# Attention and feed-forward block on one core: probabilities of the longest row of tiles transposed by DMA from SyncE

## The reference

```python
y = x * rsqrt(mean(x * x) + 1e-6) * rms_w
q, k, v = split(y @ w_in.T)                    # 8 groups: 4 x 64, 64, 64 columns each
q, k = rope(q), rope(k)
qk = where(causal, q @ k.T * 64 ** -0.5, -inf)
o = softmax(qk) @ v
x1 = layernorm(x + (x + o @ w_out.T))
x_q = ternary(x1, 0.33, 0.5)
out = layernorm(x1 + x_q @ (ternary(weight, 0.2, 0.6) + rram_variation).T)
```

## Time and profile before

| | us |
|---|---|
| median of 2 timed runs | 1411.64 (1410.79 to 1412.50) |
| the profiled execution | 1411.72 |
| its span | 1409.9 |
| TensorE busy | 1289.2 (91%) |
| VectorE busy | 1182.2 (84%) |
| ScalarE busy | 1107.8 (79%) |
| GpSimd busy | 852.2 (60%) |

### The profile page before, as it was taken

One profiled execution on the slowest core, in us unless ns is written; L12 is line 12 of the kernel. 1 busy time (PEld: TensorE's weight loads), 2 busy tenths in 40 slices (PEclk: granted clock), 3 DMA queues, 4 the chain that ended last, 5 costly groups with the idle time before them and its releaser, 6 DMA issues.

```text
span 1409.9 us, 25319 instructions
## 1 busy us (share of the span) xinstructions
PE 1289.2 (91%) x7328; PEld 755.6 (54%) x7328; DVE 1182.2 (84%) x3062; ACT 1107.8 (79%) x2327; POOL 852.2 (60%) x904
## 2 busy tenths in 40 slices
PE   4689898999989999999989999999989999898886
PEld 2455555555645555555645555555555555454554
DVE  4688887989898898988898898989898898888976
ACT  5768778788888888788888888788887788687764
POOL 1356666386746765386646766386646766786566
PEclk9799999999999999999999999999999999999998
DMA  6101111021101201021101211021101211110012
GB/s 202 26 20 48 56 31 32 27 57 46 39 21 47 59 28 31 25 59 45 38 22 42 59 33 31 24 61 43 37 24 28 71 35 44 56 42 27 19 36 82
DMA packets 45164, 61.82 MB, mean 44 GB/s; under 512 B 10465, under 2 KB 27105, under 8 KB 45025
## 3 DMA queue, kind: packets, MB, share of 16 engines
q1 hardware_dynamic: 45024, 60.20, 14.4%
HBM read 34.74 MB, written 4.46 MB: 28 GB/s over the span
## 4 chain that ended last, share of the span: by engine, by line
PE 53%; POOL 10%; DVE 9%; issue 9%; ACT 8%; DMA 7%; SPq 3%; POOLq 0%; DVEq 0%; ACTq 0%
PE s L1167 11%; PE x L1179 11%; PE t L1223 11%; PE x L1207 7%; PE ot L1138 6%; DMA spread<-recip_rows 6%; PE ot L1136 5%; ACT prob L831 4%; DVE prob L1010 3%; DVE prob_lo L1102 2%; ACT prob_hi L799 2%; POOL o_raw L766 2%; SPq L574 1%; POOL o_lo L772 1%; SPq L590 1%
## 5 line engine op out<-in xcount | busy, mean ns | idle before, releaser
L799 ACT ACTIVATE prob_hi<-t 128x512 f16<-128x512 f32 x576 | 340.3, 592 | 139.4 <-PE t L1223 134.5
L1102 DVE SCALAR_TENSOR_TENSOR prob_lo<-t,prob_hi 128x512 f16<-128x512 f32 x576 | 394.2, 685 | 59.7 <-ACT prob_hi L799 53.9
L831 ACT ACTIVATE prob<-prob,neg_max 128x896 f32<-128x896 f32 (+7 forms) x512 | 391.9, 767 | 9.3 <-DVE neg_max L1010 7.3
L1167 PE MATMUL s<-k_t,q_t 128*128 128x512 f16 (+3 forms) x1536 | 349.5, 329 | 32.7 <-DVE neg_max L1010 12.1
L1223 PE MATMUL t<-ident,prob 128*128 128x128 f32 x2304 | 350.3, 275 | 6.8 <-ACT prob L831 6.7
L1010 DVE CUSTOM_DVE_ANT_0 prob<-s,mask,score_scale 128x512 f32<-128x512 f32 (+3 forms) x512 | 319.8, 643 | 41.1 <-PE s L1167 23.9
L1223 PEld LDWEIGHTS t<-ident,prob 128*128 128x128 f32 x2304 | 289.4, 142 | 105.8 <-ACT prob L831 14.0
L1138 PE MATMUL ot<-prob_lo,v_sb 128*128 128x512 f16 x576 | 220.7, 383 | 30.2 <-DVE prob_lo L1102 29.1
L1136 PE MATMUL ot<-prob_hi,v_sb 128*128 128x512 f16 x576 | 220.1, 382 | 1.5 <-DVE o_raw L1083 0.9
L1167 PEld LDWEIGHTS s<-k_t,q_t 128*128 128x128 f16 x1536 | 137.7, 99 | 123.1 <-DVE neg_max L1010 37.6
L772 POOL TENSOR_TENSOR o_lo<-o_raw,o_hi 128x256 f16<-128x256 f32 x128 | 86.2, 674 | 194.1 <-ACT o_hi L906 192.5
(11 more groups left out here) (105 smaller groups left out, 1816.5 us busy)
## 6 DMA issues: line engine op xcount, KB each, us to landing
swapped<-flat SPq DMA_DIRECT2D x320, 64.0 KB, 2.0
spread<-recip_rows SPq DMA_DIRECT2D x128, 128.0 KB
recip_rows<-turned SPq DMA_DIRECT2D x512, 0.5 KB
raw<-L_attn_w_in SPq DMA_DIRECT2D x8, 768.0 KB, 4.2
raw<-L_attn_w_out SPq DMA_DIRECT2D x8, 512.0 KB, 3.7
out<-acc SPq DMA_DIRECT2D x16, 256.0 KB, 2.0
acc<-L_attn_x SPq DMA_DIRECT2D x3, 1024.0 KB, 9.8
acc<-L_attn_x SPq DMA_DIRECT2D x4, 256.0 KB, 3.1
```

The lines of the kernel that those rows point to most:

```text
L799: act.activation(prob_hi[:, u % 2, :], t_ps[u % 2][:, :], ACT.Copy, scale=P_SCALE).then_inc(prob_hi_done, 1)
L831: act.activation(row, row, ACT.Exp, bias=neg_max[:, kk % 4, h:h + 1], scale=-1.0, accum_out=total[:, kk % 4, h:h + 1]).then_inc(ex_done, 1)
L1102: dve.scalar_tensor_tensor(out=prob_lo[:, u % 2, :], in0=t_ps[u % 2][:, :], scalar=P_SCALE, in1=prob_hi[:, u % 2, :], op0=ALU.mult, op1=AL ...
L1167: mm = pe.matmul(s_ps[:, off:off + cols], q_t[:, h, s * P:(s + 1) * P], k_t[:, part, keys:keys + cols], start=(part == 0), stop=(part == 1))
```

## The change

For row tile s = 7 (`FAR`) of each batch, TensorE's transposes are gone. In place of them, for each head h, ACT copies the whole row of probabilities, 128x1024 float32 in SBUF, to float16 `far_hi` ("ph"); DVE writes the rest to `far_lo` ("pl"); and SP issues one transposing DMA from each, to `far_hi_t` and `far_lo_t`, eight blocks of 128x128 at a time. The products of units 28 to 35 read these. The first of them waits for all eight transfers of the batch (four heads, hi and lo). The other 28 units of a batch (the near ones) keep their path, with counts and buffers renumbered. The tables of places are as they were: "ph" and "pl" stand 2 and 4 steps behind the exponential of their head (1 and 2 for the last head).

```diff
+        if s == FAR:
+            for h in range(HG):
+                put(exps[h] + (2 if h < HG - 1 else 1), ("ph", b, h))
+                put(exps[h] + (4 if h < HG - 1 else 2), ("pl", b, h))
...
+                        elif e[0] == "ph":
+                            _, b, h = e
+                            wait(sp, far_hi_done, g, 2 * HG, b * HG + h + 1)
+                            wait(sp, pv_done, g, BODY, b * UNITS)
+                            sp.dma_start_transpose(far_hi_t[:, h, :, :], far_hi[:, h, :]).then_inc(far_hi_in, 16)
+                        elif e[0] == "pl":
+                            _, b, h = e
+                            wait(sp, far_lo_done, g, 2 * HG, b * HG + h + 1)
+                            sp.dma_start_transpose(far_lo_t[:, h, :, :], far_lo[:, h, :]).then_inc(far_lo_in, 16)
...
+                        elif e[0] == "ph":
+                            _, b, h = e
+                            wait(act, ex_done, g, 2 * NT * HG, (b * NT + FAR) * HG + h + 1)
+                            wait(act, far_hi_in, g, 32 * HG, 16 * HG * b)
+                            wait(act, far_lo_done, g, 2 * HG, HG * b)
+                            act.activation(far_hi[:, h, :], prob_row(FAR, h), ACT.Copy, scale=P_SCALE
+                                           ).then_inc(far_hi_done, 1)
...
-                            wait(dve, t_done, g, BODY, (b + back) * UNITS + first_unit(last + 1))
+                            if last == FAR:
+                                wait(dve, far_lo_done, g, 2 * HG, (b + back + 1) * HG)
+                            else:
+                                wait(dve, t_done, g, NEAR, (b + back) * NEAR_HALF + first_unit(last + 1))
...
+                        elif e[0] == "pl":
+                            _, b, h = e
+                            wait(dve, far_hi_done, g, 2 * HG, b * HG + h + 1)
+                            wait(dve, far_lo_in, g, 32 * HG, 16 * HG * b)
+                            dve.scalar_tensor_tensor(out=far_lo[:, h, :], in0=prob_row(FAR, h), scalar=P_SCALE,
+                                                     in1=far_hi[:, h, :], op0=ALU.mult, op1=ALU.subtract
+                                                     ).then_inc(far_lo_done, 1)
...
-                    wait(pe, prob_hi_done, g, BODY, u + 1)
+                    if s == FAR:
+                        wait(pe, far_hi_in, g, 32 * HG, 16 * HG * (b + 1))
+                        wait(pe, far_lo_in, g, 32 * HG, 16 * HG * (b + 1))
+                        hi, lo = far_hi_t[:, :, j, :], far_lo_t[:, :, j, :]
...
-                        wait(pe, prob_lo_done, g, BODY, u - 1)
-                        for h in range(HG):
-                            mm = pe.transpose(t_ps[u % 2][:, h * P:(h + 1) * P],
-                                              prob_row(s, h)[:, j * P:(j + 1) * P], ident[:, :])
-                        mm.then_inc(t_done, 1)
+                        if s != FAR:
+                            m = NEAR_UNITS.index(u)
+                            wait(pe, prob_lo_done, g, NEAR, m - 1)
+                            for h in range(HG):
+                                mm = pe.transpose(t_ps[m % 2][:, h * P:(h + 1) * P],
+                                                  prob_row(s, h)[:, j * P:(j + 1) * P], ident[:, :])
+                            mm.then_inc(t_done, 1)
```

More of the change, by code:

```diff
@@ L48 @@
 FIRST_TILES = 8
+FAR = NT - 1
 POOL_TILES = 14
@@ L336, in seq_block @@
         prob_lo = sb("prob_lo", [P, 2, BANK], F16)
+        far_hi = sb("far_hi", [P, HG, KEYS], F16)
+        far_lo = sb("far_lo", [P, HG, KEYS], F16)
+        far_hi_t = sb("far_hi_t", [P, HG, NT, P], F16)
+        far_lo_t = sb("far_lo_t", [P, HG, NT, P], F16)
         o_low = sb("o_low", [DH, BANK])
@@ L495, in unit_of, with unit_of_near @@
             return b, s, u - first_unit(s)
+        NEAR_UNITS = [u for u in range(BODY) if unit_of(u)[1] != FAR]
+        NEAR = len(NEAR_UNITS)
+        NEAR_HALF = NEAR // 2
+        def unit_of_near(m):
+            back, m = divmod(m, NEAR)
+            return back * BODY + NEAR_UNITS[m]
         def over_bodies(eng, one):
```

35 lines of the change are left out of this document (23 added, 12 removed).

## The result

| | before | after |
|---|---|---|
| median of 2 timed runs, us | 1411.64 (1410.79 to 1412.50) | 1573.33 (1572.17 to 1574.48) |
| span of the profiled execution, us | 1409.9 | 1572.7 |
| mean granted clock of TensorE | 0.984 | 0.919 |

The ratio is 1.1145, with a 95% interval of 1.1097 to 1.1193: 161.7 us slower, where 40 had been forecast. The direction was right; the time lies 63 us above the range.

A forecast was written before the change was run, and what follows sets the result against it. PE was taken as the bound, ACT close behind. Six middle passes at +3.2 us (first batch) and +3.6 (second) gave +40.8, the other four batches netting nothing: 1452 us from 1411.6, range 1395 to 1510.

The forecast's parts named there:

- What is removed: 128 of 576 units lose four transposes, one prob_hi, one prob_lo: PE 55 us, ACT 76, DVE 88.
- The copies' lengths: 64 far_hi on ACT at 1.02 us, total 65 us; 64 far_lo on DVE at 1.65 us, total 106 us.
- The transfers' length: SP's 128 transposing transfers: landing 3.1 us; one following another (T) near 1.2 us.
- The second path: SP's reciprocal broadcasts, middle pass's first batch: behind the last far_lo transfer, landing at 623.5 for POOL, +3.2 us.
- the first path: Longest row's data to its first product, middle pass's first batch: 5.5 us late, less 3.9 given back by PE, +1.6.
- Rival 2: Transposing transfers are dear, following one another in over 1.35 us; at 2 us the time is 1526; chance 0.19.
- Rivals 1 and 3: Gain and stall cancel, about 1420 us, chance 0.26; faster by PE's removed work, 1383 or 1356 us, chance 0.09.
- (1): PE's first product of each longest row waits 4 to 7 us on a far transfer, in 15 batches of 16.
- (2): The last 128x1024 exponential comes 3 us later relative to the units before it.
- (3): far_hi near 1.0 us, far_lo between 1.3 and 2.5, with the long ones beside POOL.
- (4): Transfers' spacing and landing; spacing over 1.35 us makes SP's swapped copies and broadcasts late and POOL wait.
- (5): PE's eight far units run at little more than their own work once the data is there.

The follow-up runs named there:

- The run with late products: Changed kernel with the longest row's eight products issued later, none in its first four slots, two in each of the last four: 1568.5 us.
- The unread transfers: Kernel before plus 128 transposing transfers of zeroed buffers that nobody reads, at the changed kernel's places: 1560.5 us (kernel before 1411.8).
- the plain copies of the same bytes: Kernel before with one unread plain 256 KB SBUF copy at each of the 128 transfer places: 1472.7 us (kernel before 1416.0).
- the other two: Kernel before with, at the same places, 128 unread transposing transfers: 1560.5 us; or four tiny unread copies at each place: 1660.1 us.
- the run without transfers: Changed kernel without its 128 transposing transfers, TensorE multiplying far_hi and far_lo unturned: 1458.1 us (kernel before 1411.8).

## Why the prediction was wrong in size

**What is removed** was about right: at most 2.1 us a batch on PE against 2.6, seen only where no data is late.

**The copies' lengths** were right or too dear: far_hi 1.05 us (1.02), far_lo 1.40 on average (1.65). What they cost was not. I pushed the last exponential by 3.1 us and let PE's idle time and savings pay for it. The data came when I said. Set against the product of unit 21 (603.32 before, 663.98 after, 60.66 apart), the last exponential ends at 617.4 in the time of the kernel before, as forecast (617.5), and the last far_lo at 620.5 (620.8). But even with no transfer to wait for, unit 28 is 4.7 us late in these batches, with no gap ahead of it: PE has stood still before, for scores that VectorE brings late because far_lo waits for far_hi ahead of them (the 3.51 us at 679.34, behind the far_lo at 677.05). I looked only at the chain of the row's own data. With the gain on PE the copies cost 46 us, more than my whole sum, before a transfer is issued.

**The transfers' length** was nearly right: landing 3.3 us (3.1), T 1.36 us (1.2). I had put the point at which the dear case starts at T = 1.35, and the trace lies on it. But the threshold was worked out from eight transfers in a row from 611 on.

**The step that failed is SP's queue, which both paths run through.** I counted when the data is ready, and priced the time from there to the issue at 0.1 us in a first batch and 1.4 in a second (a hi transfer at 0.7 with its issue, where one holds SP 1.3, and the swapped copies). In the middle passes it measured 6.3 to 6.5 us and 3.7 to 3.9. In the batch shown the first transfer goes out at 675.68, which is 615.0 in the time of the kernel before, behind two swapped copies and four stores; the weight load and the 3.03 us of the third transfer follow; and the last goes out at 626.8, not 620.9. The product comes 11.7 us late and not 5.5, and 8.7 against 6.2 in the second batches.

**The second path**, the broadcasts, is where this queue cost most, and the larger miss. The run with late products shows that the first path does not set the time. I let POOL's product start at 623.5, 3.2 us later than before, took the later of the two paths and stopped. By the queue the broadcasts go out at 628.2 and not 620.9, and the product starts at 634.3, 13.9 us late; a middle first batch as a whole became 14.6 us longer. The unread transfers show what this path costs by itself: 149 us, 9.3 a batch. Two things were left out beside the queue: POOL's product starts 5.7 to 6.0 us after the first of the two broadcasts is issued (687.09 to 692.79 with unread transfers, 688.88 to 694.92 with the change), not 2.5, and everything behind them on SP (stores, swapped copies) is late for POOL too. The second batches had no such path in my sum, and the four batches outside the middle passes, which I had put at nothing in all, took 24 us.

**Costed at nothing** was the added DMA time, with the queue's share of 14.4% as cover. By the plain copies of the same bytes, the 57 us they cost lie on the same line as the other two, so the bytes show no price of their own. The cover that mattered was SP's, and it was not there.

**PE's clock** stood in no step. I gave PE back 2.6 and 1.3 us behind unit 28 at the full clock; the row's units began at 0.69 in the first batch shown. Against the run without transfers PE is busy 42 us longer for the same work; what of this reached the time is open.

**The rivals.** Rival 2 named the right place (broadcasts and swapped copies behind the transfers, POOL waiting) but priced it by T alone: at T = 1.36 it gives 1452. The 0.9 us and the 10.5 us that were worked out beside it are both off the 1.36. Rivals 1 and 3 are out. Of the five signs, (1) the waits at the first far product came, 4.2 to 6.3 us in the middle passes, 13 of them in all and not 15; (2) and (3) held, and far_lo is long beside POOL, with 1.88 us at 677.05 where the median is 1.23; of (4) the waits of POOL came; and (5) did not: the eight units took 2.9 us more in a middle first batch and 0.4 less in a second.

## What to carry to other kernels

When a change adds DMAs, write out the issuing engine's queue with the hold of each instruction and see what is late behind them: at these places each us of hold added on SP cost 0.7 to 0.8 us, whatever it moved, while 212 us of other holds taken away brought only 36 us back. An engine of which the busy table has no line can be the bound. Whether another engine could issue the transfers at less cost was not tried. A term that ends on "the later of two paths" has to be priced on each path alone, as both may have their own chain behind them.

## What the runs showed of the hardware

- A transposing transfer of 128x1024 float16 holds SP 1.31 us and lands 3.3 us after its issue (medians of the changed kernel); of 128, 10 held it over 2 us. It moves its 256 KB in (180192 - 45024) / 128 = 1056 packets, 248 bytes each on average.
- The hold of a DMA on SP does not follow its size: 0.58 us for a copy of 0.5 KB between SBUF tensors, 0.59 for one of 64 KB, about 0.6 for 256 KB; 0.29 for the store of 0.5 KB to DRAM, 0.66 for the one store that took the place of four, and 0.37 for the weight load of 768 KB in the kernel before.
- Behind plain DMAs that have not landed, one of the first transposing transfers holds SP longer. With the weight load in flight it was 3.0 to 3.2 us in all six middle first batches of the changed kernel, each ending 0.14 to 0.25 us ahead of the load's landing; with load and broadcasts it was 5.13 us in the batch shown, ending at 668.66 where POOL could start at 668.75. That it waits for their landing fits these rows; no run was made for it alone.
- The Trainium skill (VectorE: DVE Perf Modes, The three transpose paths) has 1309 ns for one 128x128 block by DMA. Here transfers of eight blocks follow one another in 1.36 us and land after 3.3, so the figure does not add up over blocks: eight times 1309 ns, an estimate from that page, would be 10.5 us. No run here turns a single block.
